# Two gated cross-attention blocks with expert layers on one core: the second expert layer moves its rows and its outputs by scatters instead of gathers

## What is computed

```python
h = layernorm(X)                              # 1024 x 256
logits = h @ Wr.T + bias                      # 16 experts
w, idx = top2(softmax(logits)); w = w / (sum(w) + 1e-9)
for each token t and choice k:                # 2048 rows in all
    y[t,k] = (silu(h[t] @ Wg[idx]) * (h[t] @ Wu[idx])) @ Wd[idx]
shared = (silu(h @ sWg) * (h @ sWu)) @ sWd    # every token
X = X + tanh(g) * (sum_k w[t,k] * y[t,k] + shared)
```

## Time and profile before

| what | us |
|---|---|
| median of 3 runs | 540.24 (538.51 to 542.14) |
| the profiled execution, its own time | 537.9 |
| its span in the profile | 536.0 |
| PE busy in the span | 451.0 (84%) |
| DVE busy | 359.8 (67%) |
| ACT busy | 172.0 (32%) |
| POOL busy | 137.3 (26%) |

### The profile page before, as it was taken

One profiled execution on the slowest core, in us unless ns is written; L12 is line 12 of the kernel. 1 busy time (PEld: TensorE's weight loads), 2 busy tenths in 40 slices (PEclk: granted clock), 3 DMA queues, 4 the chain that ended last, 5 costly groups with the idle time before them and its releaser, 6 DMA issues.

```text
span 536.0 us, 8924 instructions
## 1 busy us (share of the span) xinstructions
PE 451.0 (84%) x2894; PEld 362.2 (68%) x2894; DVE 359.8 (67%) x925; ACT 172.0 (32%) x412; POOL 137.3 (26%) x146
## 2 busy tenths in 40 slices
PE   5699999999999999449993499999999768999800
PEld 4567766866865899438873488887799746878600
DVE  6979889888988945554545746867864476555532
ACT  3332132223212701114530235555540213444300
POOL 4925101100110000057307303122000007651073
PEclk9899999999999999559998689999999867999955
DMA  8410220220221061125635223430049103666243
GB/s 277 120 52 29 78 79 0 78 78 0 78 76 48 30 226 50 39 60 153 144 123 157 59 76 101 129 100 0 1 148 361 42 0 101 177 146 120 70 131 104
DMA packets 27424, 51.48 MB, mean 96 GB/s; under 512 B 5184, under 2 KB 16832, under 8 KB 27392
## 3 DMA queue, kind: packets, MB, share of 16 engines
q1 hardware_dynamic: 23264, 39.79, 21.9%
q0 software_dynamic: 4128, 11.28, 9.4%
HBM read 40.83 MB, written 10.22 MB: 95 GB/s over the span
## 4 chain that ended last, share of the span: by engine, by line
PE 60%; issue 15%; DVE 12%; POOL 6%; DMA 4%; ACT 1%; POOLq 0%; SPq 0%; DVEq 0%
PE ps L862 10%; PE ps L673 8%; PE ps L521 8%; PE ps L522 8%; PE ps L523 8%; PE ps L887 5%; POOL qc L502 3%; POOL probs L473 2%; PE ps L828 2%; PE ps L569 2%; PE ps L621 2%; DMA qc<-expert_rows,slot_i 2%; PE ps L579 1%; PE ps L791 1%; PE ps L872 1%
## 5 line engine op out<-in xcount | busy, mean ns | idle before, releaser
L486 POOL DMA_INDIRECT qb<-stream_rows,gather_rows x54 | 51.5, 953 | 158.9 <-DVE gather_rows L1404 137.7
L473 POOL TENSOR_TENSOR probs<-probs,rowrec 128x512 f32<-128x512 f32 x28 | 28.6, 1043 | 160.6 <-DVE rowrec L1229 160.6
L1191 DVE TENSOR_TENSOR big<-ps,big 128x512 fp32r<-128x512 f32 (+3 forms) x80 | 47.4, 633 | 21.1 <-ACT big L933 20.9
L933 ACT ACTIVATE big<-ps 128x512 fp32r<-128x512 f32 (+3 forms) x80 | 41.4, 560 | 60.5 <-PE ps L579 53.9
L862 PE MATMUL ps<-experts_s,ring 128*128 x216 | 59.2, 399 | 1.6 <-issue 1.6
L521 PE MATMUL ps<-xs_hi,A_hi 128*128 128x512 f32 x128 | 53.3, 416 | 5.3 <-DVE xs_lo L1186 5.3
L521 PE MATMUL ps<-big 128*128 128x256 f32 (+3 forms) x172 | 53.0, 308 | 0.0
L522 PE MATMUL ps<-big 128*128 128x256 f32 (+3 forms) x172 | 52.4, 305 | 0.0
L523 PE MATMUL ps<-big 128*128 128x256 f32 (+3 forms) x172 | 52.3, 304 | 0.0
L522 PE MATMUL ps<-xs_lo,A_hi 128*128 128x512 f32 x128 | 51.3, 400 | 0.0
L523 PE MATMUL ps<-xs_hi,A_lo 128*128 128x512 f32 x128 | 51.2, 400 | 0.0
(11 more groups left out here) (146 smaller groups left out, 879.6 us busy)
## 6 DMA issues: line engine op xcount, KB each, us to landing
experts_s<-ffn SPq DMA_DIRECT2D x24, 384.0 KB, 5.3
expert_rows<-G SPq DMA_DIRECT2D x54, 128.0 KB, 2.6
W<-attn SPq DMA_DIRECT2D x8, 704.0 KB, 4.1
W<-attn SPq DMA_DIRECT2D x8, 672.0 KB, 4.2
W<-attn SPq DMA_DIRECT2D x16, 320.0 KB, 4.4
stream_rows<-qb SPq DMA_DIRECT2D x16, 128.0 KB, 1.9
X<-x SPq DMA_DIRECT2D x4, 256.0 KB, 4.7
out<-X SPq DMA_DIRECT2D x8, 128.0 KB, 2.3
```

The costliest lines, as they stand in the source:

```text
L473: nc.gpsimd.tensor_tensor(part, part, rowrec[:, 4 * h:4 * h + 4, :].unsqueeze(3).to_broadcast([P, 4, 2, L]), ALU.mult).then_inc(s.p, 1)
L486: nc.gpsimd.indirect_dma_start(XG[:, u, :], None, rows_d[n], bass.IndirectOffsetOnAxis(gather_rows[:, b:b + 1], 0)).then_inc(xg_landed[u], 16)
L933: return nc.scalar.activation(dst, src, ACT.Copy)
L1191: V.tensor_tensor(dst, src, upper.bitcast(F32), ALU.subtract).then_inc(done, 1)
```

## The change

In the **first expert layer** the work stays. Two things around it differ: its ring of gathered outputs has four places instead of eight (`CG_RING`), so that POOL's gather number u waits for DVE's addition u - 3; and it runs in other places of SBUF.

In the **second expert layer**:

- Every expert gets its own region of 9 blocks of rows (`CAPACITY`) in a DRAM tensor. A token's slot is then expert x 1152 + its count so far, which no longer needs the totals. The routing goes by pairs of tiles, beside the output products: the normalisation is done four times for two tiles each; PE's transposes, router matmuls and counts for the earlier pairs stand between halves of output products 3 to 7; the last pair comes after them.
- The one-hot matrices, their matmuls, the store of rows and the gather of blocks go. POOL scatters the rows of each tile, once for each choice, from SBUF to their slots (`send_rows`, 16 indirect DMAs of 1056 bytes a row: 256 numbers, twice the token's number, its first expert).
- After the last count, 16 DMAs write 128 zero rows behind each expert's last row (`clear_rows`): SP does eight, ACT does eight. For each, the engine reads the address from SBUF into a register (`value_load`).
- SP then waits for all of these and all scatters, and loads the 31 blocks by direct DMAs, the address of each again read into a register (`load_blocks`).
- All eight shared jobs now stand ahead of the blocks. PE's first waits for the last slots (the counts use its PSUM bank); ACT's first tanh stands behind its eight zero writes in ACT's list.
- DVE works out the places of the blocks before the shared jobs (`block_places`, five operations of 128 x 496 among some twenty), and in their first passes `filled_rows`, `shifts` and `weights`. In each block's pass it runs two operations of one column more (`aim`), which give each row the place 2 x token + choice, or a spare place for rows that are padding.
- POOL scatters each block's outputs from the ring of four to those places (`send_outputs`, 31 indirect DMAs) while the loop runs. The store by SP goes. After the last, SP loads for each tile both choices at once (`load_outputs`, 8 direct DMAs of 256 KB) into buffers that are free, and the additions and stores of X follow.

The diff, cut to its core:

```diff
-XG_RING, YS_RING, CG_RING = 8, 4, 8
+XG_RING, YS_RING, CG_RING = 8, 4, 4
...
-                j.n, j.head, j.blocks = n, (0, 4)[n], NBLK[n]
-                j.all = 2 * j.head + j.blocks
+                j.n, j.head, j.blocks = n, (0, NT)[n], NBLK[n]
+                j.all = j.head + j.blocks
...
+        def clear_rows(engine, which, experts):
...
+            engine.wait_ge(*ff[1].clear_at(1))
+            for e in experts:
+                at_row = engine.value_load(clear_at[0:1, e:e + 1], min_val=0, max_val=E1 * CAPACITY * P * ROW)
+                engine.dma_start(block_rows(at_row), zero_row[:]).then_inc(cleared[which], 16)
...
+            def load_blocks():
+                j, s = jobs[1], ff[1]
+                clear_rows(sp, 0, range(CLEARED_BY_SP))
+                sp.wait_ge(cleared[0], 16 * (CLEARED_BY_SP + 1))
+                sp.wait_ge(cleared[1], 16 * (E1 - CLEARED_BY_SP))
+                sp.wait_ge(*s.rows_at(1))
+                sp.wait_ge(*s.sent(16 * 2 * NT))
+                for b in range(j.blocks):
+                    u, _ = j.landed(b, XG_RING)
+                    if b >= XG_RING:
+                        sp.wait_ge(*s.t(b - XG_RING + 1))
+                        sp.wait_ge(*s.aim(2 * (b - XG_RING + 1)))
+                    at_row = sp.value_load(row_at[0:1, b:b + 1], min_val=0, max_val=E1 * CAPACITY * P * ROW)
+                    sp.dma_start(rows_s[:, u, :], block_rows(at_row)).then_inc(xg_landed[1][u], 16)
+
+            def load_outputs():
+                j = jobs[1]
+                for b in range(j.blocks - YS_RING, j.blocks):
+                    u, landed = j.landed(b, YS_RING)
+                    sp.wait_ge(ys_landed[1][u], landed)
+                for t in range(NT):
+                    sp.dma_start(CG_PAIR[t], outputs_d[2 * t * P:2 * (t + 1) * P, :].rearrange("(p k) d -> p k d", k=2)
+                                 ).then_inc(xg_landed[1][t], 16)
...
-            store_rows(1, 0)
-            store_rows(1, 1)
-            store_blocks(1)
+            load_blocks()
+            load_outputs()
...
+            def send_rows():
...
+                for q in range(NT // 2):
+                    pool.wait_ge(*s.slots(q + 1))
+                    for t in (2 * q, 2 * q + 1):
+                        for k in range(2):
+                            nc.gpsimd.indirect_dma_start(
+                                sorted_d, bass.IndirectOffsetOnAxis(slot_i[:, t, k:k + 1].bitcast(U32), 0),
+                                rows_s[:, t, :], None).then_inc(s.sent.sem, 16)
+
+            def send_outputs():
...
+                for b in range(j.blocks):
+                    pool.wait_ge(*s.aim(2 * b + 2))
+                    pool.wait_ge(*s.y(j.evictions(b + j.head + 1)))
...
+                    nc.gpsimd.indirect_dma_start(
+                        outputs_d, bass.IndirectOffsetOnAxis(target_i[:, b:b + 1].bitcast(U32), 0),
+                        YS[:, u, :], None).then_inc(ys_landed[1][u], 16)
...
                 for t in range(NT):
+                    output(t, range(HP // 2))
+                    if n == 1:
+                        if t == 3:
+                            transpose_pair(3, 0)
+                        elif t == 5:
+                            transpose_pair(3, 1)
+                        elif t == 6:
+                            rank(1, 0)
+                        elif t == 7:
+                            router(1, 1)
+                            transpose_pair(3, 2)
+                    output(t, range(HP // 2, HP))
+                    if n == 1:
+                        if t == 3:
+                            router(1, 0)
...
+                        elif t == 7:
+                            router(1, 2)
...
+                if n == 1:
+                    rank(1, 1)
+                    rank(1, 2)
+                    transpose_pair(3, 3)
+                    router(1, 3)
+                    rank(1, 3)
+                    totals(1)
...
+                    for q in range(NT // 2):
+                        normalise_pair(l, q)
+                        whole_pair(l, q, TILE_BANKS[q % 2])
+                    clear_rows(act, 1, range(CLEARED_BY_SP, E1))
...
+            def route_and_normalise():
...
+                added(0)
+                added(1)
+                normalise(3, 0)
+                added(2)
+                added(3)
+                normalise(3, 1)
+                r.largest(0)
+                added(4)
+                added(5)
+                normalise(3, 2)
+                r.slots(0)
+                added(6)
+                r.largest(1)
+                added(7)
+                r.slots(1)
+                normalise(3, 3)
+                r.largest(2)
+                r.slots(2)
+                r.largest(3)
+                r.slots(3)
...
+                def aim(b):
+                    u, landed = j.landed(b, XG_RING)
+                    dve.wait_ge(xg_landed[n][u], landed)
+                    V.scalar_tensor_tensor(target[:, b:b + 1], first_of[:, u:u + 1], expert_of[:, b:b + 1],
+                                           token_of[:, u:u + 1], ALU.is_equal, ALU.add).then_inc(s.aim.sem, 1)
+                    dve.wait_ge(*s.aim(2 * b + 1))
+                    V.scalar_tensor_tensor(target_i[:, b:b + 1], target[:, b:b + 1], filled[:, b:b + 1],
+                                           spare[:, b:b + 1], ALU.mult, ALU.add).then_inc(s.aim.sem, 1)
...
+                    if n and up == 1:
+                        route.filled_rows()
+                    elif n and up == 2:
+                        route.shifts()
+                    elif n and up == 5:
+                        route.weights()
```

526 lines of the change are left out of this document (338 added, 188 removed).

## The result

Four runs each gave a median of 532.25 us (531.5 to 532.6) against 539.38 (536.63 to 542.14): a ratio of 0.9859, 95% interval 0.9824 to 0.9893, so 1.4% faster. The forecast was 536.8 us, with a range of 530 to 542. The profiled execution took 532.07 us with a span of 530.2, against 536.0: 5.8 us less, where the sum gave 3.4.

What follows compares the result with a forecast made beforehand. PE bounds output products and block loop; gains lay in 29 us between and 31.1 us after the last copy. 511.7 + 19.9 + 1.0 = 532.6 against 536.0, 3.4 less, so 536.8 us from median 540.24; range 530 to 542.

Steps and rivals of the forecast that it cites:

- the sum: Whole span: last copy 511.7, plus 19.9 for the end and 1.0 for the first layer, 532.6 against 536.0.
- the rows' side: Second layer from the last output product to block 0: last slots at 434.0, block 0 at 458.1, losing 10.0 us.
- The clears: Eight register-read-and-DMA steps on ACT before its first tanh: 1.2 us each, bounds 0.35 and 1.7, ACT free at 444.3.
- The free read: Rival, chance 0.25: the clears' register read costs nearly nothing, ACT is ready 5.0 us earlier, time 531.8 us.
- Shared jobs: Eight jobs from ACT's start to block 0's gate and up product: 13.8 us, two of them slow at low clock.
- The block loop: Second layer, block 0 to block 30: 49.3 us instead of 50.4, with `aim` hidden under PE's pass.
- The outputs' side: Second layer's end, from the last output copy through scatter, loads, additions and close: 19.9 us instead of 31.1.
- the ring of four: Block loop's output ring: claimed to hold, since four passes are 6.5 us and a scatter takes 1 + 3.3.
- The close: Last store and program's end after the last addition: 4.9 us, the same as in the kernel before.
- The first layer's ring: First expert layer with four buffers: POOL's gathers wait for DVE, last addition 1.0 us later, bounds 0 and 1.5.
- From the span to the time: Whole kernel: the span's 3.4 us taken off the earlier median of 540.24 us gives 536.8 us.
- within 1%, on the faster side: Whole time against before: change under about 1% (5.4 us), 0.57; faster than 534.8 had 0.36, slower than 545.6 0.07.

Runs made afterwards that it cites:

- experiment 6: Kernel before the change with PE's register read of the next block's expert moved ahead of the gate and up products: 542.85 us, ratio 1.0054 to before.
- POOL's wait: Changed kernel with POOL's large products at the start held until DVE's second chain of small operations is through: 528.59 us.
- the ring of eight: Changed kernel with eight instead of four buffers for the first layer's gathered outputs: 530.27 us.
- all twelve profiles: One profile each of the kernel before, the changed kernel and ten edited versions of either; no single time.
- the four kernels of the old kind: The kernel before, and it with a first-layer ring of four (541.03 us), PE's register read first (542.85), or POOL's large start products delayed (532.75).
- experiment 4: First layer's ring for gathered outputs, both ways: changed kernel with eight buffers instead of four, 530.27 us; kernel before with four instead of eight, 541.03 us.
- early clears: Changed kernel with the experts' whole regions cleared by SP during the first attention and no clears behind the slots: 527.31 us.

## Why the prediction was right in its order and short in its sum

The order of the second layer came out as laid out:

| | predicted | measured |
|---|---|---|
| last slots | 434.0 | 434.24 |
| first tanh | 444.3 | 444.18 |
| block 0 | 458.1 | 457.73 |
| last output copy | 511.7 | 511.45 |
| first output addition of the experts | 518.1 | 518.36 |
| last addition | 526.5 | 528.04 |
| end of span | 532.6 | 530.2 |

The predicted column leaves out the 1.0 us of the first layer, which only its last row has; the measured one has the second layer 1.2 us later than before. So the rows' side was really a little shorter than laid out. That 1.2 is near the 1.0 of the forecast is luck: the start was 3.0 us longer, which the forecast didn't have, 1.8 of that was gone again at the first gather of outputs, the ring cost 1.8 instead of 1.0, and from the first layer's last addition to the second attention's first output addition, where the clock was the faster one, 1.7 were gained.

- **The clears.** A step of 1.2 us was right (1.19), and nearly so were its parts: I took 0.5 for the issue and 0.7 for the read, and the records show 0.34 to 0.43 and 0.66 to 0.93. I had said that no row shows the read by itself; among my rows none did, but the trace of the kernel before has PE's thirty reads in the block loop (0.30 to 0.64 us, experiment 6). The free read, at 0.25 my second likeliest case, fell, and it was ill put: with the reads gone the row of issues still takes 6.5 us, because a bound that the prediction didn't have, full DMA engines, comes in. The Trainium skill, "DMA: Bandwidth & Descriptors", section "Latency and other measured facts", gives `tensor_load` a floor of about 600 ns; the record of the load alone goes below that in this trace (0.27 us at the least), while from its start to the issue it is never under 0.66.
- **Shared jobs.** 13.8 us from the first tanh were predicted, 13.55 measured. With POOL's wait it took 451.90 - 439.90 = 12.0, with the ring of eight 12.4, at the same code: in the changed kernel the granted clock is still at 1.2 GHz from 448 to 450 and averages 0.74 in the next 2 us, so that three gate and up products behind the first tanh are slow (0.63 us a matmul instead of 0.38), where I had two slow jobs; with POOL's wait two are, and the clock is full 4.1 us behind the first tanh.
- **The block loop.** 49.3 predicted, 48.65 measured (457.73 to 506.38). Every pass but the first (1.74) and the last (1.41) took 1.63 us; with `aim` and POOL's scatter in it nothing was late, and the waits for the register read are gone. That they would go I had not said; by experiment 6 the reads there take 0.30 us instead of 0.45, and why is open.
- **The outputs' side.** From block 30's first product to the last copy's end it was 5.07 us against 4.3: the last two copies waited 1.66 us for a scatter to land, so that the ring of four, which I had said would hold, did not at the very end; it cost nothing, because POOL's row of scatters was later still. The copy to the first addition took 6.91 us against 6.4. The step that I missed is POOL's pace: five scatters at 1.28 us stand behind PE's faster drain, and the last starts 1.83 us behind its copy, not 0.2; its landing (2.4) and the first load (2.6) were shorter than the 3.3 and 2.9 that I took, which hides most of it. Sixteen additions took 9.7 us against 8.4; behind the first they are 8.73 / 15 = 0.58 apart, not 0.52, and the second waited 0.46 for the first.
- **The close.** This term was mis-sized: "Close 4.9", carried over from before, measured 2.14 (528.04 to 530.18). That is 2.7 us, more than the 2.4 by which the span is below the sum. In both kernels DVE's last addition releases the last store of 128 KB. What the other 2.7 us of before were is in the records of the program's closing line: each engine ends with an instruction named DRAIN, and the other engines' last records stand behind POOL's. First the kernel before, then the changed one:

```profile
L64 POOLq EVENT_SEMAPHORE  x2: 17/17/17, 535.8 to 535.9; - x2
...
L64 POOLq DRAIN  x1: 14487/14487/14487, 521.3 to 521.3; - x1
...
L64 SPq DRAIN  x1: 7/7/7, 533.0 to 533.0; - x1
```

```profile
L72 POOLq DRAIN  x1: 9195/9195/9195, 512.2 to 512.2; - x1
```

Before, POOL's DRAIN ends at 535.75, 2.7 us behind SP's, and the span ends 0.2 later. In the changed kernel it ends at 521.36, 8.6 us ahead of SP's (529.97). In all twelve profiles it ends 7.1 us behind the end of POOL's last indirect DMA instruction. So the close was not a constant: it was this tail of POOL's gathers, and the change took it off the path by ending POOL's work with the scatters. It goes with the change: from the last addition to the span's end it is 4.8 to 4.9 us in the four kernels of the old kind, and 2.1 in the eight of the new. The end as a whole, 18.7 us against 19.9, is thus partly errors that cancel: 0.5 and 1.3 too little in the two steps ahead, 2.8 too much here.
- **The first layer's ring.** 1.0 predicted, 1.8 to 2.1 measured in the two pairs of experiment 4. I counted the wait of the thirteenth gather alone; the sixth and seventh waited too, and the thirteenth for 1.42 us.
- **From the span to the time.** The forecast stood on the median of three runs, 540.24. In the runs of all sessions before lay between 533.73 and 542.14, with medians of 537.78 to 540.07. The interval of the ratio says how little the third digit means.

The forecast of "within 1%, on the faster side" with 0.57 was one step too timid: faster by over 1% had 0.36. With the close as it was measured the forecast would have been 534.0, below the bound of 534.8 that I had set.

## What to carry over

A single DMA issue in the trace (0.35 us) is no price for a row of them. Two queues that each issued eight clears of 132 KB did so every 0.4 to 0.5 us only until the DMA engines were full, and then every 1.16, which is about the time of the bytes; with an address read from memory a step was over 1 us from the start. So count both, the instructions of a step and its bytes. Eight such preparations ahead of an activation were 9 us of that engine's path; do them early, even at nine times the bytes, or on an engine nobody waits for. Look also at what an engine does when its work is over: in the kernel before, POOL closed only 7.1 us behind its last indirect DMA, and the span ended with it. Work that is moved from behind a loop to ahead of it costs what it takes unless something ahead was idle; look at what holds the first pass before splitting it. And before a change of one per cent is judged by whole times, cut the traces at points that the change doesn't touch: here the start alone varied by 4.2 us (34.25 to 38.48) between kernels with the same code in it.

## What I had not expected of the hardware

- **Small operations of DVE beside large ones of POOL.** DVE operations of 128 x 4 elements took 2.07 to 2.37 us instead of 0.15 when they began within a large product of POOL (128x1024, 2.4 us). Which ones meet differs from kernel to kernel by tenths: two in before, three in the changed kernel. The two normalisations of 128x256 beside POOL took 2.81 us together in the kernel with POOL's wait, against 0.73 where POOL was idle (those at 7.82 us of the changed kernel), while products of 128x512 that read PSUM kept their 0.68 us. The Trainium skill, "SBUF — State Buffer", section "SBUF: two separate sides", says that the two engines share one pair of ports, which whoever starts first holds for its whole instruction; it counts DVE's operation when that has two SBUF inputs or runs in a two-port mode. By that rule, the trace agrees: each stretched operation began within a product of POOL and ended with it (14.53 + 2.26 = 16.79 against 14.40 + 2.37 = 16.77), and one that began 0.02 us ahead of a product kept its 0.17 (19.16 against 19.18). Operations with one tensor as input were stretched as well (2.30 us at 17.25 with early clears); whether they ran in such a mode no row shows.
- **The clock at the second attention's output.** After the same pause of some 2 us in PE's products, six kernels ran the next ones at 2.4 GHz (0.39 us for 512 columns) and six began them at 1.2 GHz (0.63 us), 1.6 us apart between changed kernel and kernel before. Here the timeline of PE in the changed kernel and in the one with eight buffers:

```profile
389.29 0.39 PE L616 MATMUL ps<-big 128*128 128x512 f32 x1
```

```profile
387.38 0.63 PE L617 MATMUL ps<-big 128*128 128x512 f32 x1
```

What decides between them stays open; neither the ring nor the change does so alone (experiment 4).
- **POOL's closing DRAIN.** It ended 7.1 us behind POOL's last indirect DMA instruction in all twelve profiles, whether that was a gather or a scatter, and in the four kernels of the old kind the span ended with it.
- **An indirect store costs about what an indirect load does.** POOL started one every 1.28 us (a gather every 1.25), and it landed in 2.4 us (median) against 3.0 for the gathers of rows.
